# ScalarE takes one of two maxima banks out of PSUM: a copy beside VectorE's reduction

## The reference, cut to what matters

```
x = x + attention(layernorm(x));  x = x + ffn(layernorm(x))
scores = einsum('bhid,bhjd->bhij', qr, kr) * HD ** -0.5     # qr, kr: rotated q and k
probs  = softmax(scores, axis=-1)
out    = einsum('bhij,bhjd->bhid', probs, v)
```

## Time and profile before

| what | value |
|---|---|
| median of three runs | 1621.9 us |
| profiled execution: time, span | 1622.87 us, 1621.1 us |
| TensorE matmul busy | 1538.8 us, 95% |
| GpSimd busy | 1351.4 us, 83% |
| VectorE busy | 1130.3 us, 70% |
| ScalarE busy | 798.8 us, 49% |
| mean granted TensorE clock | 0.983 of full |

### The profile page before, as it was taken

How to read it: one execution, slowest core, us unless ns; L and a number is a source line. 1 busy time by engine, 2 the same in 40 slices (tenths; PEclk the granted TensorE clock), 3 DMA queues, 4 the chain that set the end, 5 groups by cost and what they waited for, 6 DMA issues and landing times.

```text
span 1621.1 us, 24839 instructions
## 1 busy us (share of the span) xinstructions
PE 1538.8 (95%) x9257; PEld 787.8 (49%) x9257; DVE 1130.3 (70%) x1376; ACT 798.8 (49%) x1197; POOL 1351.4 (83%) x793
## 2 busy tenths in 40 slices
PE   3699999999999999999999999999999999998677
PEld 1345454544445554544554555544454454554355
DVE  4777776676767777776677677666677767763787
ACT  1255555654554565645555555554554555554222
POOL 4589899888888999988888889988888899975774
PEclk9899999999999999999999999999999999999798
DMA  4111111111111111111111111111111111100001
GB/s 130 44 28 47 47 39 47 47 42 40 35 47 39 42 47 47 39 47 47 42 28 47 47 34 47 47 39 47 47 42 37 37 47 34 42 17 22 7 14 33
DMA packets 69191, 67.04 MB, mean 41 GB/s; under 512 B 26512, under 2 KB 52432, under 8 KB 69072
## 3 DMA queue, kind: packets, MB, share of 16 engines
q1 hardware_dynamic: 69072, 65.46, 16.0%
HBM read 29.25 MB, written 2.62 MB: 20 GB/s over the span
## 4 chain that ended last, share of the span: by engine, by line
PE 90%; DVE 8%; issue 2%; ACT 0%; DMA 0%; DVEq 0%; ACTq 0%
PE po L1100 29%; PE st L1087 24%; PE mx L1140 13%; PE ms L1123 8%; PE ms L1166 4%; PE ms L1111 4%; PE ms L1157 4%; DVE negmax L845 1%; PE mx L1225 1%; PE ms L1148 1%; PE st L1225 1%; DVE probs L802 1%; DVE st L796 1%; DVE probs L992 0%; DVE sin_part L868 0%
## 5 line engine op out<-in xcount | busy, mean ns | idle before, releaser
L845 DVE TENSOR_REDUCE negmax<-mx 128x2 f32<-128x1024 f32 x504 | 616.3, 1223 | 407.6 <-PE mx L1140 407.5
L374 POOL TENSOR_TENSOR psum_keys<-psum_keys,probs 128x1024 f32<-128x1024 f32 x256 | 608.0, 2375 | 103.9 <-ACT probs L629 84.7
L629 ACT ACTIVATE probs<-st 128x1024 f32<-128x1024 f32 x512 | 496.6, 1022 | 248.8 <-PE st L1087 246.7
L1100 PE MATMUL po<-probs,v 128*64 128x512 f32 x2048 | 495.9, 605 | 0.0
L1140 PE MATMUL mx<-keys_hi,queries_hi 64*128 64x512 f32 x1008 | 246.7, 485 | 3.9 <-DVE negmax L845 3.8
L1100 PEld LDWEIGHTS po<-probs,v 128*64 128x64 f32 x2048 | 124.2, 136 | 255.5 <-issue 152.0
L1087 PE MATMUL st<-queries_hi,keys_lo 64*128 64x512 f32 x1024 | 203.3, 392 | 0.0
L1087 PE MATMUL st<-queries_lo,keys_hi 64*128 64x512 f32 x1024 | 202.7, 391 | 0.0
L1087 PE MATMUL st<-queries_hi,keys_hi 64*128 64x512 f32 x1024 | 202.2, 390 | 0.0
L1140 PEld LDWEIGHTS mx<-keys_hi,queries_hi 64*128 64x128 f32 x1008 | 94.4, 184 | 207.7 <-issue 117.1
L374 POOL TENSOR_TENSOR psum_keys<-probs 128x1024 f32<-128x1024 f32 x64 | 152.1, 2376 | 48.2 <-ACT probs L629 48.0
(11 more groups left out here) (158 smaller groups left out, 1600.2 us busy)
## 6 DMA issues: line engine op xcount, KB each, us to landing
kq<-sin_part SPq DMA_DIRECT2D x256, 128.0 KB, 2.3
rsum<-recips SPq DMA_DIRECT2D x128, 128.0 KB, 2.9
wqkv<-in_L_attn_w_qkv_dram SPq DMA_DIRECT2D x32, 192.0 KB, 2.8
resid<-in_L_attn_x_dram SPq DMA_DIRECT2D x4, 512.0 KB, 8.2
wout<-in_L_attn_w_out_dram SPq DMA_DIRECT2D x32, 64.0 KB, 2.6
out_dram<-resid SPq DMA_DIRECT2D x8, 256.0 KB, 2.3
sums<-sums_kept SPq DMA_DIRECT2D x64, 4.0 KB
spread<-sums SPq DMA_DIRECT2D x64, 4.0 KB, 1.6
```

The costliest lines, as they stand in the source:

```text
L374: nc.gpsimd.tensor_tensor(psum_keys[:, c], first, probs[:, (STEPS * P + i) % RING], ALU.add)\
L629: nc.scalar.activation(probs[:, step_n % RING], st[step_n % 2][:, :], ACT.Exp, scale=SCALE)\
L845: nc.vector.tensor_reduce(negmax[:, t // HALF, :, t % HALF, half], banks[:, :], AX.X, ALU.max, negate=True)\
L1100: last = mm(po[HD * a:HD * a + HD, :], v[:, P % 2, KEY_ORDER[jt], HD * a:HD * a + HD], probs[:, step_n % RING, a], start=(jt == 0), stop=( ...
```

## The change

In the double steps whose number u of the first maxima unit is in `COPIED` (u = 0, 2, 6, 8, 10, 14: the double steps 2, 3, 5, 6, 7 and 1), for every pair but the first, ScalarE copies the second head's bank of `mx` to `max_copy` in SBUF. VectorE reduces the first head's bank from PSUM, counts `mx_free`, waits for the copy and reduces that. TensorE's second maxima unit waits for both. On ScalarE the copy is the first instruction of its double step, but for the double steps 3 and 7, whose copy is put at the end of 2 and 6, ahead of the spreading. `rsum` shrinks to one half, and its broadcast waits for the normalisation before it (`n` for `n - 1`).

```diff
+COPIED = (0, 2, 6, 8, 10, 14)
...
-    rsum = sb("rsum", [PART, TOKENS])
+    rsum = sb("rsum", [PART, CH])
+    max_copy = sb("max_copy", [PART, CH])
...
+    def copies_before(N, u):
+        return len(COPIED) * (N - 1) + sum(n < u for n in COPIED) if N > 0 else 0
+    def copied(N, u):
+        return N > 0 and u in COPIED
... SyncE, return_reciprocals
-            wait(sp, norm_done, n - 1)
+            wait(sp, norm_done, n)
             for a in range(2):
-                sp.dma_start(rsum[HD * a:HD * a + HD, bass.ts(c, CH)],
+                sp.dma_start(rsum[HD * a:HD * a + HD, :],
... GpSimd, normalise
-            nc.gpsimd.tensor_tensor(t, t, rsum[:, bass.ts(c, CH)], ALU.mult).then_inc(norm_done, 1)
+            nc.gpsimd.tensor_tensor(t, t, rsum[:, :], ALU.mult).then_inc(norm_done, 1)
... ScalarE
+        def copy_maxima(N, u):
+            wait(act, copy_reduced, copies_before(N, u))
+            act.wait_ge(mx_full, 16 * N + u + 1)
+            nc.scalar.activation(max_copy[:, :], mx[:, 1], ACT.Copy).then_inc(max_copied, 1)
+        def copy_ahead(P, d):
+            N, u = maxima_at(P, d, 0)
+            if present(N) and copied(N, u):
+                copy_maxima(N, u)
...
             for d in range(JT):
+                if d not in (3, 7):
+                    copy_ahead(P, d)
                 if present(P):
                     exp(P, 2 * d)
...
                     if kind == "B":
+                        copy_ahead(P, d + 1)
                         spread_maxima(X, u)
... VectorE, row_maxima
+            out = negmax[:, t // HALF, :, t % HALF, half]
+            if not copied(N, u):
+                nc.vector.tensor_reduce(out, banks[:, :], AX.X, ALU.max, negate=True).then_inc(mx_free, 1)
+                return
+            nc.vector.tensor_reduce(out[:, 0:1], banks[:, 0], AX.X, ALU.max, negate=True).then_inc(mx_free, 1)
+            dve.wait_ge(max_copied, copies_before(N, u) + 1)
+            nc.vector.tensor_reduce(out[:, 1:2], max_copy[:, :], AX.X, ALU.max, negate=True).then_inc(copy_reduced, 1)
         def max_columns(N, c):
             dve.wait_ge(mx_free, 16 * N + (16 if c else 10 if N == 0 else 8))
+            wait(dve, copy_reduced, copies_before(N, 16 if c else 8))
... TensorE, max_scores
                 wait(pe, mx_free, 16 * N + u)
+                if u > 0 and copied(N, u - 1):
+                    pe.wait_ge(max_copied, copies_before(N, u))
```

More of the change, by code:

```diff
@@ L163, in block_program @@
     maxcol_done = sem("maxcol_done")
+    max_copied, copy_reduced = sem("max_copied"), sem("copy_reduced")
     st_ps, exp_done, pv_ps, key_sum = sem("st_ps"), sem("exp_done"), sem("pv_ps"), sem("key_sum")
@@ L844, in row_maxima @@
             dve.wait_ge(mx_full, 16 * N + u + 1)
-            nc.vector.tensor_reduce(negmax[:, t // HALF, :, t % HALF, half], banks[:, :], AX.X, ALU.max, negate=True)\
-              .then_inc(mx_free, 1)
+            out = negmax[:, t // HALF, :, t % HALF, half]
[5 more added lines that the diff above has]
+            nc.vector.tensor_reduce(out[:, 1:2], max_copy[:, :], AX.X, ALU.max, negate=True).then_inc(copy_reduced, 1)
         def max_columns(N, c):
             dve.wait_ge(mx_free, 16 * N + (16 if c else 10 if N == 0 else 8))
+            wait(dve, copy_reduced, copies_before(N, 16 if c else 8))
             nc.vector.tensor_reduce(maxcol[:, c].rearrange("p (a k) -> p a k", a=2)[:, :, 0:HALF], negmax[:, c], AX.X,
```

## The result

The changed kernel takes 1607.2 us (median of four runs, 1607.01 to 1608.73) against 1622.34: a ratio of 0.9911, 95% interval 0.9895 to 0.9926. The profiled execution took 1607.2 us, span 1605.4. The forecast was 1605, range 1592 to 1619.

What follows compares the result with a forecast made beforehand. TensorE's stream was taken as the bound. Per head pair 4 x 0.19 − 2 x 0.10 = 0.56 us, times 31 = 17.4 us off, giving 1605 us; 80% range 1592 to 1619.

Steps and rivals of the forecast that it cites:

- The exposed release: TensorE's second maxima matmul: waiting for VectorE's reduction costs 0.19 us per double step, 35.3 us over 186 places.
- Both releases come in time: Second maxima matmul: VectorE's and ScalarE's releases both come before TensorE wants its load, with 0.2 to 0.4 us to spare.
- VectorE's extra work off the path: Split reductions add 0.14 us each, 26 us over the kernel, but cost nothing because VectorE idles 407.5 us.
- The spreading moved behind the copy: Double steps 3 and 7: ms returns at the unit's old start, so no 0.19 us gain and +0.10 us each.
- rsum: SyncE's broadcast of the reciprocals waits for the previous normalisation, over 13 us away: zero cost.
- A: Rival: the spreading in double steps 3 and 7 costs nothing or even gains; 1586 to 1598 us; chance 0.16.
- B: Rival: a satisfied second wait costs the second maxima matmul another 0.07 us; 1618 us; chance 0.12.
- C: Rival: K unit of double step 3 and O unit of 7 start 0.54 us late; slower, 1632 us; chance 0.08.
- D: Rival: a wait elsewhere, on GpSimd or VectorE's rotation, takes back TensorE's gain; 1620 to 1624 us; chance 0.05.
- E: Rival: the two instructions on VectorE become the bound, adding 26 us; 1649 us; chance 0.02.

Runs made afterwards that it cites:

- e6: Kernel before the change, with VectorE reducing the two banks of the same 186 units in two instructions and no copy; 1633.21 us, ratio 1.0066.
- e4: Changed kernel with the copy put ahead of four normalising ScalarE instructions in six double steps; 1598.25 us, ratio 0.985 to the kernel before.
- e1: Changed kernel with the copies of double steps 3 and 7 left out; 1604.46 us, ratio 0.9891 to the kernel before.
- e3: Changed kernel with the four spreading instructions cut in two halves around the copy of double steps 3 and 7; 1589.81 us, ratio 0.9798 to the kernel before.
- e7: Kernel before the change with only the smaller rsum buffer and its broadcast's later wait; 1622.92 us, ratio 1.0000.
- e2: Changed kernel with the copies of double steps 3 and 7 put behind the spreading; 1617.11 us, ratio 0.9967 to the kernel before.

## Why the prediction was right, step by step

- **The exposed release.** Priced at 0.19 us in the four free double steps; it is 0.19 to 0.22, since the unit starts at 2.04 (2.07 in 5) and not at 2.06. 26.0 us instead of 23.6. e6 shows the mechanism from the other side.
- **Both releases come in time.** True in the ordinary double steps, false in six. The prediction looked at ScalarE's queue in double step 5 of one pair and found the po copy and the exponentials; it did not ask what the queue holds in the pairs in which a next or a finished sequence is prepared (`normalise_x`, `normalise_y`). That costs 7.0 us, shown by e4. It is the one step that failed in its mechanism.
- **VectorE's extra work off the path.** Right but for three masked double steps 0, 0.44 us each (1.3 us); they are behind VectorE's `y_exp` instruction, whose length goes by what GpSimd does beside it. The prediction asked whether VectorE had idle time enough, and not what else stands in its queue.
- **The spreading moved behind the copy.** The release was forecast at the old start of the unit, with +0.10 us for an exposed weight load. The place is right (e1: worth nothing; e3: 15 us once `ms` returns in time), and the unit starts at 2.29 where the prediction had 2.3 (2.25 and +0.10 would be 2.35). Mis-sized is the exposure: the double steps grow by 0.03 and 0.04, not 0.10, 2.2 us instead of 6.2. Their growth is the later start of the unit and nothing more: from the unit to the next first maxima matmul it is 2.92 us in double step 3 (2.93 before) and 2.96 in 7, as before, although the load is now exposed. The 0.11 us was read off the maxima matmul of the earlier trace rows and does not hold for the K and O units; why they differ no run shows.
- **rsum.** Zero, as e7 shows.
- **The rivals.** A is out, since the spreading did decide in 3 and 7. B is out: with two waits that are met the second matmul starts at 1.72 to 1.74, no later than the stream's pace (1.50 + 0.23). C's unit start of 2.7 did not come; e3 and e1 show that its mechanism is there, at 0.04 us where C had 0.54. D and E are out by the time, 1607.2 us, and by the waits.

By the places' sum the errors partly cancel: +2.4 for the release, +4.0 for the smaller exposure, −8.3 for the nine places make −1.9 us, the distance from the forecast gain of 17.4 to the 15.5 found. That the total came out so near is luck in this part; by the total alone the forecast looks better than its steps.

The Trainium skill (VectorE: DVE Perf Modes, Rules for kernel authors) advises, for elementwise work on a matmul's output, a copy out of PSUM only where many operations follow. By that rule, carried over to a reduction, this copy is a loss; here the trace and e6 decide against it, since what the copy buys is not VectorE's time but the bank's.

## What to carry to other kernels

Where an in-order TensorE stream waits for a PSUM bank, price the time from full bank to release, not the reader's load: every 0.1 us of it can be 0.1 us of the kernel while the reader idles. Giving half of the reading to another engine makes that engine's queue part of TensorE's path, so list everything that ever stands ahead of the new instruction in that queue, in the rare stages too, and what is queued behind it and holds another bank. If the new instruction must wait, cut the work behind it and put as much in front as fits into the wait.

## What was not expected of the hardware

When ScalarE's copy is the last of the second maxima matmul's two releases, the matmul starts 0.14 us after the copy's end (644.90 to 645.04, and 706.81 to 706.95 in e2, where it is so in all 60 places of pairs 1 and later), while after VectorE's reduction in the earlier trace rows it was 0.05 us, and 0.05 for the K unit after the spreading (702.42 to 702.47). A second wait that is already met shows no cost at all, one that ends last about 0.09 us. The Trainium skill (Perfetto Trace Analysis, Identifying Dependency Chains) says that a wait on several engines may be put into extra semaphore instructions ahead of the instruction; that would fit. That ScalarE signals can't be the whole of it, since it is also ScalarE's spreading that releases the K unit in 0.05 us; no run here isolates the second wait.

A reduction of 128x512 takes 691 ns from PSUM and 686 ns from SBUF, so the reader gained nothing from the copy's place.

The `y_exp` instruction on VectorE, 128x512 in SBUF, takes 0.37 to 0.43 us at some places and 0.97 to 3.29 us at others. In all ten traces each of the long ones ends 0.28 to 0.29 us after the GpSimd instruction that was under way when it began: it behaves as if it waited for GpSimd, though the kernel puts no semaphore between the two there.
